# Three points per unit for the side work of loops 0 and 2, and an earlier route for the last group but one

## The chip, the cores and the metric

The kernel is one program on one core of a Trainium2 chip. Its time is the device time in microseconds (us) of that core. The engines are TensorE (PE in the profile, its weight loads PEld), VectorE (DVE), ScalarE (ACT), GpSimd (POOL) and the queue of SyncE (SP); they run in parallel, each executes its own instructions in order, and they wait for each other by semaphores.

## The reference

The input is x of 4 sequences x 1024 tokens x 128 channels. Six residual layers follow each other, each on a layer norm of x:

```
x = x + 0.5 * channel_mix(layernorm(x))          # RWKV-like, with the token before
x = x + attention(layernorm(x))                  # 16 heads of 8, rotary, softmax
x = x + 0.5 * channel_mix(layernorm(x))          # the same weights again
x = x + 0.5 * moe(layernorm(x))                  # 8 experts, top 2, hidden 256
x = x + linear_attention(layernorm(x))           # 16 heads of 8, causal sums, softplus
x = x + 0.5 * moe(layernorm(x))                  # the same experts again
```

moe: an RMS norm, router scores (tokens x 8), the two best experts with softmax weights, for each `(u * silu(gate)) @ w_down`, and the weighted sum plus the skip.

## The kernel before

**Tiles, groups, halves.** The 4096 tokens are 32 tiles of 128; 4 tiles are a group (8 groups), 4 groups a half (2 halves). x stays in on-chip memory all the time. Each of the two expert layers is worked in two halves, so there are four rounds r = 0 to 3 (r = 0 and 1 for the first layer, 2 and 3 for the second; the half is r % 2).

**One round.** First the *route*: `rroot` (VectorE: inverse roots of the variances, some 14 small operations in a chain), `rnorm` (VectorE: the normalised tokens xr, tile by tile), then for each group `rext` (TensorE transposes xr, ScalarE copies the result) and `rscore` (TensorE: router scores, VectorE copies them). With all four groups there come the *slots*: `rtop` 0 and 1 (VectorE: first and second expert), `rcount` (TensorE counts, VectorE copies and scans), `rscan`, `rplace` (VectorE: the slot of each token), `roff` (the expert of each slot tile) and `rweight`. Then 32 *scatters* (`scat`): GpSimd writes xr, tile by tile and twice, to its slots in HBM, sorted by expert (L1594). Then the *expert loop* of the round: 39 slot tiles, two per unit, so 20 units (`UNITS`), and three more passes to drain. Last 32 gathers (`gath`, L1604), which take the results back; they and the additions `cadd` lie in the next round's loop, or in the linear stage, or at the end.

**The expert loop** is software-pipelined over `UNITS + 3` = 23 passes. In pass u TensorE transposes unit u (L1649; it needs SyncE's load of the slots, three units ahead), does the up-projections of unit u - 1 (L1659), transposes the hidden values of unit u - 2 (L1671) and does the down-projection of unit u - 3 (L1685). VectorE copies and scales the transposed unit (L1726) and multiplies by the SiLU of unit u - 1 (L1733); ScalarE does SiLU (L1760) and the copies L1766 and L1773; SyncE stores unit u - 3 (L1828) and loads (L1822). All loads of a round wait on SyncE for all scatters of that round, and come behind the stores of the round before in its queue.

**Side pieces.** What doesn't belong to the experts is cut into pieces, and `plan_loop` writes out, before the program is built, which piece stands where: two places in a pass, `first` behind the transposition of unit u and `second` behind the up-projections. Every engine walks through the same plan and executes its own share of a piece in its place, so a piece on TensorE that needs VectorE's share of an earlier piece holds up all that TensorE has behind it. `turn_of(works, 4)` takes the next piece of each list of work at a place, with at most one piece for TensorE. All side pieces that use a PSUM bank use bank 1 (`SIDE_BANK`), one after the other.

Loop 0 carries, in this order: the end of the attention (`div`, `turn`, `proj`, `rest`, `stats`), `factors` and the channel mix of the last group (`side_mix(11)`: mn, mt, md, mx, mk, mr, mv, ms), then `route_part(1, 1, 8)` (root and norm of tiles 8 to 15 of the half, rext and rscore of groups 2 and 3), the slots of round 1 and its scatters, one per place; what is left at the last place goes there all together. By this plan rplace of round 1 stands in pass 12, and 12 of the 32 scatters stand in the last place. Loop 2 carries `route_part(3, 1, 8)`, the slots of round 3 and its scatters: rplace in pass 5, the last scatter in pass 21. `pool_follow` makes a gather or scatter wait for the transposition or up-projection of its place, in the drain passes only where there is one.

**The linear stage** (`plan_linear`, 132 steps) lies between loops 1 and 2, with a plan of its own; its `extra` pieces, at most one route piece per step, carry the route of round 2 and groups 0 and 1 of round 3. `spread` leaves empty steps behind some kinds. TensorE executes `extra` in front of the step's weighted sums (L1975), which ScalarE copies (L2169) for the division (L1917, L1922) of a later step. Its last `lstats` (the statistics of the last group) comes right before loop 2.

## Time and profile before

| | us |
|---|---|
| median of 3 runs | 1353.01 (1352.94 to 1354.49) |
| the profiled execution | 1355.71 |
| its span | 1353.80 |

| engine | busy us |
|---|---|
| TensorE matmul | 1091.2 |
| ScalarE | 806.7 |
| VectorE | 655.0 |
| GpSimd | 375.7 |

Times in the rows are counted from the span's start. Loop 0 begins near 668, loop 1 near 781, the linear stage near 860, loop 2 near 1146 and loop 3 near 1233. "Idle before <- releaser" says how long an engine sat before an instruction and what ended that; "issue" is a wait for nothing that the profile shows, "remote" or "another core or an unknown queue" one that it can't name. The granted clock of TensorE is given as a share: 1.00 is 2.4 GHz, 0.50 is 1.2 GHz, and a stretch between them is a mix of both.

### The profile page before, as it was taken

How to read it: one execution, taken by the hardware profiler on the slowest of the kernel's cores; microseconds unless marked ns; L12 is line 12 of the kernel's file. 1: busy time of each engine (PE TensorE's matmuls, PEld its weight loads, DVE VectorE, ACT ScalarE, POOL GpSimd, SP SyncE). 2: the span in 40 equal slices, each digit the busy share in tenths (PEclk: the TensorE clock that was granted, in tenths of full speed). 3: DMA queues.
4: the chain of work that ended last, by engine and by line, in shares of the span. 5: the costliest groups of instructions: out<-in, count | busy, mean ns of one | idle time of the engine just before them, and what ended most of it. 6: DMA issues, size and time to landing. Idle time of an engine off the chain costs nothing.

```text
span 1353.8 us, 20967 instructions
## 1 busy us (share of the span) xinstructions
PE 1091.2 (81%) x7616; PEld 508.4 (38%) x7616; DVE 655.0 (48%) x2060; ACT 806.7 (60%) x1164; POOL 375.7 (28%) x376
## 2 busy tenths in 40 slices
PE   3459899989989999999879489877887777898940
PEld 2332222223222321232256356443544344565630
DVE  5742555464454340433165146567666662633522
ACT  4328778788887999989734345654443331364520
POOL 2100111112100102333002744144240363155535
PEclk8779989999999999999999789889788686898985
DMA  4450450450038301100012233100000011133522
GB/s 138 62 90 1 70 83 1 71 81 2 2 54 149 102 3 62 68 15 28 9 43 69 80 90 100 34 15 19 9 17 1 13 33 40 49 112 100 143 66 67
DMA packets 83411, 74.07 MB, mean 55 GB/s; under 512 B 11248, under 2 KB 77680, under 8 KB 82416
## 3 DMA queue, kind: packets, MB, share of 16 engines
q1 hardware_dynamic: 73824, 55.06, 18.8%
q0 software_dynamic: 8192, 16.79, 4.3%
q8 instruction: 66, 1.08, 0.4%
q10 hardware_dynamic: 1296, 0.86, 0.2%
q14 instruction: 33, 0.27, 0.1%
HBM read 39.26 MB, written 33.42 MB: 54 GB/s over the span
## 4 chain that ended last, share of the span: by engine, by line
PE 53%; DVE 20%; ACT 11%; issue 5%; POOL 3%; DMA 2%; another core or an unknown queue 1%; SPq 0%; POOLq 0%; DVEq 0%; ACTq 0%
PE ps L987 11%; PE ps L1659 9%; ACT attn_probs L1250 9%; PE ps L972 6%; PE ps L1685 4%; PE ps L590 3%; PE ps L881 2%; PE ps L1962 2%; PE ps L1671 2%; POOL moe_back L1604 2%; PE ps L1649 1%; PE ps L1886 1%; DVE lin_scores L2091 1%; DVE moe_xr L1105 1%; DVE room L1106 1%
## 5 line engine op out<-in xcount | busy, mean ns | idle before, releaser
L1250 ACT ACTIVATE attn_probs<-ps 128x1024 f32<-128x1024 f32 x512 | 486.1, 1083 | 91.3 <-PE ps L972 91.2
L987 PE MATMUL ps<-attn_probs,attn_v 128*18 128x512 f32 x2048 | 275.1, 610 | 1.9 <-DVE room L1217 1.3
L972 PE MATMUL ps<-stack 50*128 50x512 bf16 x1024 | 167.3, 391 | 17.6 <-DMA stack<-row_maxima 11.5
L1594 POOL DMA_INDIRECT slots<-moe_xr,moe_slot x128 | 124.9, 975 | 197.5 <-ACT attn_probs L1250 78.9
L1659 PE MATMUL ps<-stack,lin_scores 128*128 x312 | 155.4, 621 | 0.0
L1604 POOL DMA_INDIRECT moe_back<-results,moe_slot x128 | 123.6, 966 | 111.0 <-PE ps L1649 47.2
L972 PEld LDWEIGHTS ps<-stack 50*128 50x128 bf16 x1024 | 34.3, 94 | 255.5 <-ACT attn_probs L1250 228.8
L1760 ACT ACTIVATE lin_scores<-ps 128x256 f32<-128x256 f32 x156 | 58.4, 381 | 105.6 <-PE ps L1659 100.3
L1733 DVE TENSOR_TENSOR lin_scores<-ps,lin_scores 128x256 f32<-128x256 f32 x156 | 59.1, 419 | 105.0 <-ACT lin_scores L1760 85.3
L1685 PE MATMUL ps<-stack,lin_scores 128*128 x624 | 86.6, 283 | 10.3 <-ACT lin_heads_out L1773 6.8
L1685 PEld LDWEIGHTS ps<-stack,lin_scores 128*128 128x128 f32 x624 | 78.7, 198 | 12.2 <-issue 11.9
L1288 POOL TENSOR_TENSOR room<-room 128x512 f32<-128x512 f32 x16 | 24.5, 1530 | 190.4 <-DVE room L1082 190.4
L1659 PEld LDWEIGHTS ps<-stack,lin_scores 128*128 128x128 f32 x312 | 56.1, 201 | 40.1 <-issue 40.0
L1726 DVE TENSOR_SCALAR lin_scores<-ps,c_norm_scale 128x256 f32<-128x256 f32 x80 | 37.9, 474 | 56.2 <-PE ps L1649 49.7
L2091 DVE TENSOR_TENSOR lin_scores<-ps,c_causal 128x512 f32<-128x512 f32 x64 | 41.1, 684 | 49.4 <-PE ps L1962 46.7
L2161 ACT ACTIVATE lin_scores<-ps 128x512 f32<-128x512 f32 x64 | 34.8, 595 | 45.7 <-PE ps L1962 45.5
L987 PEld LDWEIGHTS ps<-attn_probs,attn_v 128*18 128x18 f32 x2048 | 34.8, 96 | 71.8 <-issue 48.4
L1082 DVE SCALAR_TENSOR_TENSOR room<-ps,c_attn_b,moe_xr 128x512 f32<-128x512 f32 x32 | 23.7, 748 | 78.6 <-PE ps L881 77.1
L1649 PE MATMUL ps<-c_ident,moe_gathered 128*128 128x128 f32 x156 | 33.5, 297 | 29.1 <-DMA moe_gathered<-slots 17.3
L1766 ACT ACTIVATE lin_scores<-ps 128x512 f32<-128x512 f32 x80 | 46.7, 584 | 15.2 <-PE ps L1671 9.7
L1671 PEld LDWEIGHTS ps<-c_ident,lin_scores 128*128 128x128 f32 x312 | 39.4, 144 | 37.5 <-issue 36.5
L1773 ACT ACTIVATE lin_heads_out<-ps 128x256 f32<-128x256 f32 x80 | 30.1, 377 | 37.2 <-PE ps L1685 22.4
(237 smaller groups left out, 1584.4 us busy)
## 6 DMA issues: line engine op xcount, KB each, us to landing
stack<-qk_parts SPq DMA_DIRECT2D x48, 256.0 KB, 9.2
moe_gathered<-slots SPq DMA_DIRECT2D x76, 128.0 KB
results<-lin_heads_out SPq DMA_DIRECT2D x76, 128.0 KB
slots<-zeros SPq DMA_DIRECT2D x2, 2496.0 KB, 14.9
qk_parts<-moe_xr SPq DMA_DIRECT2D x32, 128.0 KB, 5.2
qk_parts<-moe_xr SPq DMA_DIRECT2D x16, 192.0 KB, 2.8
stack<-in_expert_w SPq DMA_DIRECT2D x1, 3072.0 KB
x<-in_x SPq DMA_DIRECT2D x8, 256.0 KB, 8.4
```

The source lines that it names most:

```text
L972: instruction = T.matmul(k.ps[:, SCORE_BANKS[i % 3][s], :], d.stack[b % 2][rows, 1, pair, kt * P:(kt + 1) * P], d.stack[b % 2][rows, 0, pa ...
L987: instruction = T.matmul(k.ps[32 * j:32 * j + STRIP, PV_BANK, :], d.v[:, b % 2, kt, first:first + STRIP], d.probs[:, n % A_PROBS, j * BANK ...
L1250: A.activation(d.probs[:, n % A_PROBS, 2 * e * BANK:2 * (e + 1) * BANK], k.ps[:, banks[0]:banks[1] + 1, :].rearrange("p a n -> p (a n)"), ...
L1594: G.indirect_dma_start(out=k.dram["slots"][half], out_offset=bass.IndirectOffsetOnAxis(ap=d.slot[:, s, at, c:c + 1], axis=0), in_=d.xr[:, ...
L1604: G.indirect_dma_start(out=k.back[:, at % RING, c, :], out_offset=None, in_=k.dram["results"][half], in_offset=bass.IndirectOffsetOnAxis(a ...
L1649: instruction = T.transpose(k.ps[:, bank, i * P:(i + 1) * P], k.moe.gathered[:, u % NG, i, :], k.ident[:, :])
L1659: T.matmul(k.ps[:, bank, :], d.gt[:, u % NB, i, :], w[:, bass.ds(offset[u, i], 2 * HIDDEN)], start=True, stop=True).then_inc(k.full[bank], 1)
L1671: instruction = T.transpose(k.ps[:, bank, at:at + P], d.h[:, u % NB, i, c * P:(c + 1) * P], k.ident[:, :])
L1685: instruction = T.matmul(k.ps[:, bank, i * DIM:(i + 1) * DIM], d.ht[:, u % NB, i, c * P:(c + 1) * P], w[:, 2 * HIDDEN + c * DIM:][:, bass. ...
L1733: V.tensor_tensor(d.h[:, u % NB, i, :], k.ps[:, bank, 0:HIDDEN], d.silu[:, u % NB, i, :], ALU.mult).then_inc(k.free[bank], 1)
L1760: A.activation(d.silu[:, u % NB, i, :], k.ps[:, bank, HIDDEN:2 * HIDDEN], ACT_FN.Silu).then_inc(k.e_silu, 1)
L2091: V.tensor_tensor(d.scores[:, m % NS, :].rearrange("p (j t) -> p j t", j=HPG), k.ps[:, bank, :].rearrange("p (j t) -> p j t", j=HPG), caus ...
```

## The change

Loops 0 and 2 get three places per pass for the pieces: the third stands behind the transposition of the hidden values, in front of the down-projection, on TensorE and ScalarE; VectorE and SyncE execute it right behind the second. Loops 1 and 3 keep two. Scatters stay at the first two places. In loop 0 the route of group 2 of the half becomes a work list of its own that starts behind `proj`, beside the last mix; group 3 comes behind the mix, each with its own root (4 tiles). In the linear stage group 2 of round 3 gets its route behind `lstats` of group 6, and loop 2 starts with the route of group 3 alone. By the new plan rplace of round 1 stands in the second place of pass 7 and 3 scatters in the last place that takes any; in loop 2 rplace stands in the third place of pass 2 and the last scatter in pass 18. `rnorm` now names its first and last tile.

```diff
-SIDE_BANK = 1
+SIDE_BANK, PLACES = 1, 3
...
-    yield OTHER, ("rnorm", r, part)
+    yield OTHER, ("rnorm", r, part * TPB, (part + 1) * TPB)
...
+def route_group(r, g):
+
+    yield OTHER, ("rroot", r, g * TPG, (g + 1) * TPG)
+    yield OTHER, ("rnorm", r, g * TPG, (g + 1) * TPG)
+    yield PRODUCT, ("rext", r, g)
+    yield PRODUCT, ("rscore", r, g)
...
+        if ("lstats", GROUPS - 2) in out:
+            routes += spread(route_group(3, HALF_GROUPS - 2))
...
-    slots = [[] for _ in range(2 * (UNITS + 3))]
+    places = [[[] for _ in range(PLACES)] for _ in range(UNITS + 3)]
+    slots = [place for unit in places for place in unit[:2]]
...
-        works = [list(route_part(3, 1, TPB)) + list(route_slots(3))]
+        works = [list(route_group(3, HALF_GROUPS - 1)) + list(route_slots(3))]
...
+    for n, out in enumerate(place for unit in places for place in unit) if r % 2 == 0 else ():
+        out += turn_of(works, 4)
+        if n % PLACES < 2:
+            out += scatters if n // PLACES == UNITS + 2 and n % PLACES else scatters[:1]
+            scatters = scatters[1:]
+        if ("stats", BATCH - 1, HALVES - 1) in out:
+            works.insert(0, [(OTHER, ("factors", TILES - TPG, TILES))] + list(side_mix(SIDE_MIXES - 1)))
+        if ("proj", BATCH - 1, HALVES - 1) in out:
+            works.append(list(route_group(1, HALF_GROUPS - 2)))
+        if ("ms", SIDE_MIXES - 1) in out:
+            assert not works
+            works.append(list(route_group(1, HALF_GROUPS - 1)) + list(route_slots(1)))
+        if ("rplace", r + 1) in out:
+            scatters = transfers("scat", r + 1)
     for n, out in enumerate(slots):
-        if r == 0 or r == 2:
-            out += turn_of(works, 4)
-            out += scatters if n == len(slots) - 1 else scatters[:1]
...
-            if ("ms", SIDE_MIXES - 1) in out:
-                works.append(list(route_part(1, 1, TPB)) + list(route_slots(1)))
...
-            for at in range(piece[2] * TPB, (piece[2] + 1) * TPB):
+            for at in range(piece[2], piece[3]):
...
@@ TensorE, and ScalarE likewise: def pe_loop, def act_loop
-        first, second = k.e_plan[r][u]
+        first, second, third = k.e_plan[r][u]
...
             turn_hidden(u - 2)
+        for piece in third:
+            side(piece)
         if 0 <= u - 3 < UNITS:
             down(u - 3)
...
@@ VectorE, and SyncE likewise: def dve_loop, def sp_loop
-        for piece in second:
+        for piece in second + third:
             side(piece)
```

## Rows read from the trace of the kernel before

**Rows 1.** The page, busy time, share of the span and instructions of each engine.
```profile
PE 1091.2 (81%) x7616; PEld 508.4 (38%) x7616; DVE 655.0 (48%) x2060; ACT 806.7 (60%) x1164; POOL 375.7 (28%) x376
```

**Rows 2.** Table by stretch: length; busy PE, PEld, DVE, ACT, POOL; clock, DMA share, GB/s.
```profile
667.89:756.33 88.44, 76.39 (x387) 53.20 (x388) 47.70 (x168) 39.00 (x93) 19.27 (x20) 0.92 0.21 58
756.33:780.91 24.58, 4.96 (x31) 3.72 (x29) 0.70 (x2) 2.68 (x7) 16.64 (x18) 0.65 0.24 77
1124.00:1146.45 22.45, 16.52 (x117) 11.93 (x117) 3.87 (x15) 3.58 (x6) 7.64 (x9) 0.61 0.16 47
1146.45:1223.39 76.94, 67.28 (x350) 45.35 (x350) 38.80 (x130) 38.62 (x92) 29.28 (x31) 0.91 0.27 79
1223.39:1232.68 9.29, 4.45 (x30) 3.31 (x29) 0.71 (x2) 2.72 (x7) 2.79 (x3) 0.93 0.36 105
```

**Rows 3.** Chain of waits behind loop 0: start, duration, what.
```profile
765.55 3.81 another core or an unknown queue
769.69 0.33 SPq L1828
770.09 8.72 issue
```

**Rows 4.** Timeline of GpSimd, loop 0: start, duration, instruction, idle before it.
```profile
733.66 1.18 POOL L1594 DMA_INDIRECT slots<-moe_xr,moe_slot  x1 [32.96 <-DVE moe_slot L1510]
741.13 0.95 POOL L1594 DMA_INDIRECT slots<-moe_xr,moe_slot  x1 [1.24 <-remote]
762.68 0.96 POOL L1594 DMA_INDIRECT slots<-moe_xr,moe_slot  x1 [0.30 <-issue]
776.57 0.95 POOL L1594 DMA_INDIRECT slots<-moe_xr,moe_slot  x1 [0.30 <-issue]
```

**Rows 5.** Timeline of TensorE, loop 0.
```profile
707.78 0.66 PE L590 MATMUL ps<-c_ident,moe_xr 128*128 128x128 f32 x4 [2.62 <-DVE moe_xr L1456]
708.27 2.75 PE L1659 MATMUL ps<-stack,lin_scores 128*128 x4
725.40 0.23 PE L1419 MATMUL ps<-moe_both,before_bf 128*128 128x128 bf16 x1 [1.74 <-DVE moe_both L1481]
749.90 0.38 PE L1649 MATMUL ps<-c_ident,moe_gathered 128*128 128x128 f32 x2
750.12 1.88 PE L1659 MATMUL ps<-stack,lin_scores 128*128 x4
753.17 0.27 PE L1649 MATMUL ps<-c_ident,moe_gathered 128*128 128x128 f32 x1
```

**Rows 6.** Timeline of VectorE, loop 0.
```profile
703.03 0.16 DVE L1445 TENSOR_SCALAR moe_root_var<-moments 128x8 f32<-128x8 f32 x1
706.62 2.14 DVE L1456 TENSOR_SCALAR moe_xr<-x,moments,moe_root 128x128 f32<-128x128 f32 x8
723.44 0.28 DVE L1472 TENSOR_REDUCE moe_top<-moe_scored 128x16 f32<-128x128 f32 x1
725.26 0.17 DVE L1482 TENSOR_TENSOR moe_gap<-moe_top 128x16 f32<-128x16 f32 x1
```

**Rows 7.** Timeline of VectorE, then of TensorE, end of the linear stage.
```profile
1126.91 0.20 DVE L2042 TENSOR_TENSOR lin_total<-ps,lin_total 128x36 f32<-128x36 f32 x1 [2.15 <-remote]
1131.59 2.40 PE L1975 MATMUL ps<-lin_scores,lin_v 128*9 128x128 f32 x32
```

**Rows 8.** Timeline of TensorE, start of loop 2.
```profile
1154.42 1.11 PE L590 MATMUL ps<-c_ident,moe_xr 128*128 128x128 f32 x4 [3.20 <-DVE moe_xr L1456]
1155.32 3.62 PE L1659 MATMUL ps<-stack,lin_scores 128*128 x4
1158.74 1.42 PE L1410 MATMUL ps<-router_scaled,moe_xrt 128*128 128x8 f32 x8
1169.39 0.23 PE L1419 MATMUL ps<-moe_both,before_bf 128*128 128x128 bf16 x1 [1.74 <-DVE moe_both L1481]
```

**Rows 9.** Timeline of TensorE, seam behind loop 2.
```profile
1227.00 1.15 PE L1685 MATMUL ps<-stack,lin_scores 128*128 x8 [1.02 <-issue]
```

More of the change, by code:

```diff
@@ L474, in plan_loop @@
     scatters = []
-    for n, out in enumerate(slots):
-        if r == 0 or r == 2:
-            out += turn_of(works, 4)
-            out += scatters if n == len(slots) - 1 else scatters[:1]
-            scatters = scatters[1:]
-            if ("stats", BATCH - 1, HALVES - 1) in out:
-                works.insert(0, [(OTHER, ("factors", TILES - TPG, TILES))] + list(side_mix(SIDE_MIXES - 1)))
-            if ("ms", SIDE_MIXES - 1) in out:
-                works.append(list(route_part(1, 1, TPB)) + list(route_slots(1)))
-            if ("rplace", r + 1) in out:
-                scatters = transfers("scat", r + 1)
-        elif r == 1 and ("lnorm", 0) in [piece for one in slots[:n] for piece in one]:
+    for n, out in enumerate(place for unit in places for place in unit) if r % 2 == 0 else ():
[12 more added lines that the diff above has]
+            scatters = transfers("scat", r + 1)
+    for n, out in enumerate(slots):
+        if r == 1 and ("lnorm", 0) in [piece for one in slots[:n] for piece in one]:
             if k.l_more[0][1][0] not in ("lexp", "lln") or n >= 2 * (UNITS + 1):
                 out.append(k.l_more.pop(0)[1])
-    assert not works and (r != 2 or ("rweight", 3) in [piece for one in slots for piece in one])
-    plan = [(slots[2 * u], slots[2 * u + 1]) for u in range(UNITS + 3)]
-    k.e_plan[r] = plan
+    assert not works and (r % 2 or ("rweight", r + 1) in [piece for unit in places for one in unit for piece in one])
+    k.e_plan[r] = places
     for u in range(UNITS + 3):
-        first, second = plan[u]
+        first, second, third = places[u]
         if u < UNITS:
@@ L506, in plan_loop @@
             k.banks.fill(("eht", r, u - 2), 6)
+        for piece in third:
+            if key := bank_key(piece):
+                k.banks.fill(key, SIDE_BANK)
         if 0 <= u - 3 < UNITS:
@@ L1704, in pe_loop @@
             turn_hidden(u - 2)
+        for piece in third:
+            side(piece)
         if 0 <= u - 3 < UNITS:
@@ L1736, in dve_loop @@
     for u in range(UNITS + 3):
-        first, second = k.e_plan[r][u]
+        first, second, third = k.e_plan[r][u]
         if u < UNITS:
@@ L1776, in act_loop @@
     for u in range(UNITS + 3):
-        first, second = k.e_plan[r][u]
+        first, second, third = k.e_plan[r][u]
         for piece in first:
@@ L1785, in act_loop @@
             turn_hidden(u - 2)
+        for piece in third:
+            side(piece)
         if 0 <= u - 3 < UNITS:
@@ L1839, in sp_loop @@
     for u in range(UNITS + 3):
-        first, second = k.e_plan[r][u]
+        first, second, third = k.e_plan[r][u]
         if u + AHEAD < UNITS:
@@ L1846, in sp_loop @@
             store(u - 3)
-        for piece in second:
+        for piece in second + third:
             side(piece)
```

## The prediction

> **What bounds the kernel now.** I read the page's line of busy shares first: TensorE is busy 81% of the span, so a microsecond in which it waits in order is lost unless something else hides it [rows 1]. Then the table by stretches, for the two loops that change [rows 2]. Loop 0 runs from its first transposition (667.89) to its last pair of up-projections (756.33), 88.44 us for 20 units; loop 2 takes 76.94 us for the same 20. A unit without a stall takes 3.27 us, the distance of two starts of L1649 [rows 5], so 20 take 65.4: loop 0 carries 23.0 us of stalls, loop 2 11.5. Third, the seam behind each loop: 24.58 us from the last up-projections of loop 0 to the first transposition of loop 1, with TensorE busy 4.96 of them; behind loop 2 the seam is 9.29 us [rows 2]. The chain of waits says what the longer seam waits for: 8.72 us from 770.09, which end at 778.81 when the gather of loop 1 is issued [rows 3]. That gather needs every scatter of the second half, and GpSimd issues the last at 776.57, one each 1.263 us since 762.68 ((776.57 - 762.68) / 11) [rows 4]: twelve scatters have no place left in the loop and stand in its last one. Loop 2 has none left over.
>
> **The change, part by part.** By the lists of both plans, the last placing of the route (rplace) of loop 0 moves from unit 12 to unit 7, its 32 scatters begin at unit 8 instead of 12 and still go two per unit; 3 instead of 12 are left in the last place. In loop 2 rplace moves from unit 5 to 2 and the last scatter from unit 21 to 18. I sum against the profiled execution, 1355.71 us (span 1353.80 and 1.91 around it); it is 2.70 above the median of 1353.01, so I add the sum to the median.
>
> *A. The seam of loop 0.* Nine scatters fewer at its end, 9 x 1.263 = 11.4 us [rows 4]. Behind them comes a second limit: ScalarE's last three copies of the down-projection end waits of up to 3.8 us put down to an unknown queue, while scatters are issued without a pause [rows 3]. The last store leaves at 769.7, 9.1 us before the gather of 778.81; if those waits stay whole, the gather can't come earlier than about 770.1 in the old clock of events, which is 8.7. The pauseless stream now ends at about 766, so the third wait should shrink. Gain 8.6 to 11.4; I take 10.0.
>
> *B. The length of loop 0.* The work moved is the same, but each engine executes in order, and a unit now holds three links of a chain that crosses engines. TensorE meets the same waits with fewer units between them to cover them. The present waits of the route: 2.62 us before L590, 1.74 before L1419 [rows 5]. Now by hand. Unit 1 has, on VectorE, one root (2.9 us: from 703.03 to the rnorm at 706.62, less a multiplication of 0.7 [rows 6]), a multiplication with SiLU, the statistics, and half of an rnorm (1.1 us, half of 2.14 [rows 6]) before TensorE's rext of the same unit: TensorE, free at about 676.4, waits until 681.3, and the mix of the last group, whose factors come behind that on VectorE, is transposed at 686.8 instead of 684.2. From there the mix has three places per unit and gains: its last TensorE step comes at 696.0 instead of 697.6, but in unit 4 and not 6. The last group's root and rnorm then hold rext to 705.8 (a wait of 3.4), and unit 6 begins at 709.1, or at 710.8 if TensorE falls to its lower clock behind the wait, as it did behind the 2.62: L1659 took 2.75 us there for four matmuls that take 1.88 otherwise [rows 5]. In unit 6 TensorE needs both tops before rcount: 0.4 + 0.5 + 1.95 + 0.7 + 1.85 = 5.4 us from the unit's start (a top is 723.44 to 725.43 [rows 6]), though it has only 2.8 us of its own work before it. From there VectorE is the bound for two units: rcount, rscan, rplace and roff are about 6.6 us, with two transposed copies and one multiplication between them 8.2, so unit 9 begins 13.6 us after unit 6, 722.8 to 724.5. Eleven units of 3.27 and the stall behind the first five scatters (GpSimd itself sat 1.24 us at 741.13 [rows 4]; 1.1 us of the unit, kept) bring the last up-projections to 759.9 to 761.6 instead of 756.33. First scatter: near 722.5, not 733.66. Loss 3.6 to 5.3; bounds 2.0 (all later waits half as long) and 6.5 (each wait over 2.6 us costs a stretch of the lower clock too); I take 4.6.
>
> *C. The linear stage.* It gets root, rnorm, rext and rscore of the last group but one, 1, 3, 6 and 8 steps behind the statistics. VectorE is idle 2.15 us before L2042 at 1126.91 and its consumer on GpSimd stands behind a scatter until 1128.2, so root and rnorm are hidden [rows 7]. TensorE's are not: rext falls into the run of L1975 at 1131.59 that ScalarE's next copy waits for, rscore into the run behind it, and TensorE is at its lower clock in this stretch (granted 0.61, near half [rows 2]). The lower-clock prices are 1.1 us (L590) and 1.42 (L1410) [rows 8]. Cost 2.5; bounds 0 (both fit into idle time of TensorE, of which the 22.45 us have 5.9) and 3.0.
>
> *D. The length of loop 2.* Gone is the second rext and rscore, which stood in a unit only 0.7 us over the plain one. Added is the same crowding, and here the chain starts cold. rext runs at 1154.4 as before, but then come turn(1) (0.65) and rscore (1.42) before the first up-projections, which start at 1157.7 instead of 1155.32 and end near 1160.7. VectorE can only then multiply (1161.9) and take both tops (3.9): rcount goes at 1165.9, and TensorE, having only one transposition in between, waits 5 us; before, it had units 2 and 3 there and waited 1.74, at 1169.39 [rows 8]. rcount thus comes 3.5 us earlier in time and two units earlier in work (6.5 us). Behind it VectorE runs multiplication, rscan, rplace and turn(3) until 1174.5, which holds turn(4). A stall-free unit 4 would have been reached at 1174.5 - 4 x 3.27 = 1161.4 on the scale of unit 0; before, the same scale stands at 1156.8 when the route is through. Cost 4.7; bounds 1.5 (VectorE's small operations slip between, no lower clock) and 5.5.
>
> *E. The seam of loop 2.* The last nine scatters now are long done, so the 1.02 us that TensorE sat before L1685 at 1227.00 [rows 9] should go. Gain 0.7; bounds 0 and 1.0.
>
> Loops 1 and 3, the fourth variable in the plan and the rnorm's new arguments issue the same instructions: nothing. All else that moves (ScalarE's copies of rext, 0.6 us each) lies in its idle time, 49 of 88 us in loop 0 [rows 2].
>
> Sum: -10.0 + 4.6 + 2.5 + 4.7 - 0.7 = +1.1 us: 1356.8 as a profiled execution, 1354.1 as a median.
>
> The clock belongs in B and D. The row shows half-rate matmuls after a wait of 2.62 us (2.75 for 1.88) [rows 5] and after one of 3.2 us (3.62 [rows 8]). The Trainium skill, page "TensorE: Matmul & The Clock Gate", section "Loop structure matters more than you think", says that long waits between matmuls drop the engine to its half rate, and that the loop nest decides it; it speaks against a change that trades many short waits for few long ones, and this trace agrees. With full rate behind every wait B and D would be about 1.7 and 1 us smaller and the sum -1.6.
>
> GpSimd's first scatter, beside VectorE's roff, lasted 1.18 us and the others 0.95 to 0.96 [rows 4]. The Trainium skill, "DMA: Bandwidth & Descriptors", section "SWDGE vs HWDGE vs iDMA", says that VectorE in one of its modes can lock GpSimd out of the memory where it writes its descriptors. Fewer scatters now lie behind the last VectorE route step, so this could only shorten A's stream, by 0.2 us.
>
> **Rivals.** *The waits are covered.* The seam gives its full measure and the crowding little: A -10.7, B +2.0, C +1.0, D +1.5, E -0.7, together -6.9: 1346.1. For it: loop 0 is 23.0 us over plain units, and part of that is one chain that three places run faster. Against it: no added place gives VectorE any time, and in unit 11 it was already the one waited for.
>
> *TensorE's in-order wait for rcount* (slower). In both loops it stands one place behind the second top, with 2.4 to 5 us of nothing under it, and each such wait brings the lower clock: B +6.5, C +3.0, D +5.5, with A at -8.6 and E at -0.4, together +6.0: 1359.0. It decides as soon as B + C + D exceed the seam by 2.7, that is 13.4. For it: L1659's 3.62 us behind the wait at loop 2's start. Against: the wait of 1.74 had no slow matmuls behind it.
>
> *The seam isn't the scatters'* (the change doesn't do what it says): the unexplained waits of ScalarE grow with the loop's later end and eat A down to 5: sum +6, the same time as the last.
>
> **How the numbers follow.** About 0.2%, 2.7 us, is what a measurement of this kernel tells from no change. The forecast has 0.42 (0.34 within 2.7 us, 0.03 faster, 0.05 slower), the covered waits 0.31 (0.29 faster, 0.02 within), the rcount wait 0.20 and the seam's failure 0.07 (0.25 slower, 0.02 within). Faster 0.32, same 0.38, slower 0.30. The forecast's own range is 1350 to 1358; with the two sides down to 1345.5 and up to 1360.5 some 0.2 is left out.
>
> **What would show it.** Last scatter of loop 0 at about 770 and the first transposition of loop 1 at 774 to 778 (A and B together); the last up-projections at 760 to 762 (B); a wait over 2.3 us before L1419 in both loops (B, D); the linear stage's end at 1149 less the shift of before (C); loop 2 near 81.6 us (D). Wrong it would be if L590 in unit 1 of loop 0 waits under 3 us, or if the seam behind loop 0 stays above 18 us.

## The result, and the profile after

The changed kernel takes 1359.49 us (median of 8 runs, 1358.14 to 1366.59), the kernel before beside it 1354.41 (8 runs, 1351.61 to 1359.86): ratio 1.0038, 95% interval 1.0020 to 1.0057. It is slower by 0.4%, 5.1 us by the medians. The forecast was 1354.1 and a sum of +1.1 us; its own range was 1350 to 1358, and only the wide one, with the rivals' sides, reached to 1360.5. The profiled execution after took 1358.14 us, with a span of 1356.2 and a mean granted clock of 0.896, that of before 1355.71, 1353.8 and 0.896: +2.4 in both.

The table by stretches of the kernel after, with the columns of [rows 2]: loop 0, its seam, the end of the linear stage, loop 2 and its seam.

```profile
666.52:763.92 97.40, 81.47 (x387) 55.65 (x388) 51.65 (x184) 39.23 (x93) 27.78 (x29) 0.86 0.20 59
763.92:778.51 14.59, 4.76 (x30) 3.52 (x28) 0.71 (x2) 2.79 (x7) 8.06 (x9) 0.80 0.30 91
1119.83:1142.36 22.53, 15.82 (x128) 11.98 (x128) 7.55 (x34) 4.18 (x7) 7.33 (x8) 0.68 0.15 47
1142.36:1226.18 83.82, 69.73 (x339) 45.78 (x339) 37.92 (x125) 37.88 (x91) 31.97 (x33) 0.86 0.26 75
1226.18:1234.66 8.48, 4.45 (x31) 3.31 (x29) 0.70 (x2) 2.69 (x7) 0.00 (x0) 0.94 0.29 84
```

Against [rows 2] these rows show a trade between stages: loop 0 is 8.96 us longer (97.40 for 88.44), its seam 9.99 shorter, loop 2 6.88 longer (83.82 for 76.94), its seam 0.81 shorter. The end of the linear stage, from its last group of score matmuls to loop 2, took 21.98 us before (1124.47 to 1146.45) and takes 22.53. The rest, which the prediction put at nothing, gave 3.6 back: 1.37 ahead of loop 0, 2.07 in loop 1 (74.77 to 72.70) and 0.17 in the rest of the linear stage; loop 3 and the end took 0.42. Together +2.4. The five stages that the change touches add up to +5.6.

In loop 0 TensorE does the same 387 matmuls, but in 81.47 us and not in 76.39: the granted clock of the stretch fell from 0.92 to 0.86. In loop 2 it does 339 for 350, since a group's route has left, and yet is busy 69.73 us for 67.28, at a clock of 0.86 for 0.91. TensorE's timeline in loop 0, at the last group's route:

```profile
699.99 1.88 PE L1676 MATMUL ps<-stack,lin_scores 128*128 x4
705.43 1.12 PE L607 MATMUL ps<-c_ident,moe_xr 128*128 128x128 f32 x4 [3.56 <-DVE moe_xr L1473]
711.30 3.60 PE L1676 MATMUL ps<-stack,lin_scores 128*128 x4
718.05 0.23 PE L1436 MATMUL ps<-moe_both,before_bf 128*128 128x128 bf16 x1 [2.72 <-DVE moe_both L1498]
718.18 2.05 PE L1702 MATMUL ps<-stack,lin_scores 128*128 x8
720.44 2.44 PE L1676 MATMUL ps<-stack,lin_scores 128*128 x4
724.27 1.88 PE L1676 MATMUL ps<-stack,lin_scores 128*128 x4
```

The four up-projections of a unit (L1676) take 1.88 us at full clock. Behind the wait of 3.56 us they take 3.60, and the down-projections (L1702) 2.05 for 1.06. The granted clock is 0.50 over the 9.28 us from 705.43 to 714.71 and 0.63 over the 4.55 us behind the second wait, and 1.00 only from 722.73 on. Loop 2's start shows the same, and answers to [rows 8]:

```profile
1150.23 1.11 PE L607 MATMUL ps<-c_ident,moe_xr 128*128 128x128 f32 x4 [7.24 <-DVE moe_xr L1473]
1153.82 3.76 PE L1676 MATMUL ps<-stack,lin_scores 128*128 x4
1162.60 0.29 PE L1436 MATMUL ps<-moe_both,before_bf 128*128 128x128 bf16 x1 [4.59 <-DVE moe_both L1498]
1162.80 3.78 PE L1676 MATMUL ps<-stack,lin_scores 128*128 x4
```

The extension (L607, the transposition of the route's xr) waits 7.24 us where TensorE waited 3.48 before unit 1's transposition at 1150.56 and 3.20 before the extension; that is 0.6 us more. The count (L1436) waits 4.59 where it waited 1.74. The count is 6.8 us earlier in time, 2.7 if counted from the loop's first transposition, and yet loop 2 takes longer.

### The profile page after: what moved, and what is told of

It is laid out like the page before. It is cut to its first block, busy times and chain, and to the rows that moved or that the text cites. A ratio compares the mean times of both kernels' runs of the same rounds, so it can differ in the third digit from the quotient of the medians.

```text
span 1356.2 us, 20999 instructions
## 1 busy us (share of the span) xinstructions
PE 1095.4 (81%) x7616; PEld 509.6 (38%) x7616; DVE 661.7 (49%) x2092; ACT 807.1 (60%) x1164; POOL 376.5 (28%) x376
## 3 DMA queue, kind: packets, MB, share of 16 engines
q8 instruction: 66, 1.08, 0.4%
## 4 chain that ended last, share of the span: by engine, by line
PE 53%; DVE 21%; ACT 11%; issue 5%; POOL 3%; DMA 2%; another core or an unknown queue 1%; SPq 0%; POOLq 0%; DVEq 0%; ACTq 0%
PE ps L1004 11%; PE ps L1676 9%; ACT attn_probs L1267 9%; PE ps L989 6%; PE ps L1702 4%; PE ps L607 3%; PE ps L898 2%; PE ps L1983 2%; POOL moe_back L1621 2%; PE ps L1688 2%; PE ps L1666 2%; PE ps L1907 1%; DVE lin_scores L2112 1%; DVE moe_xr L1122 1%; PE ps L1943 1%
## 5 line engine op out<-in xcount | busy, mean ns | idle before, releaser
L989 PE MATMUL ps<-stack 50*128 50x512 bf16 x1024 | 167.5, 391 | 17.5 <-DMA stack<-row_maxima 11.4
L1676 PE MATMUL ps<-stack,lin_scores 128*128 x312 | 159.5, 635 | 0.0
L1702 PE MATMUL ps<-stack,lin_scores 128*128 x624 | 85.8, 281 | 8.8 <-issue 4.9
L1702 PEld LDWEIGHTS ps<-stack,lin_scores 128*128 128x128 f32 x624 | 77.8, 196 | 10.5 <-issue 10.5
L1676 PEld LDWEIGHTS ps<-stack,lin_scores 128*128 128x128 f32 x312 | 57.6, 206 | 41.3 <-issue 41.2
L607 PE MATMUL ps<-c_ident,room 128*128 128x128 f32 x132 | 25.9, 329 | 29.2 <-DVE room L596 18.2
```

The costliest lines, as they stand in the source:

```text
L607: instruction = T.transpose(k.ps[:, bank, i * P:(i + 1) * P], source(i), k.ident[:, :])
L989: instruction = T.matmul(k.ps[:, SCORE_BANKS[i % 3][s], :], d.stack[b % 2][rows, 1, pair, kt * P:(kt + 1) * P], d.stack[b % 2][rows, 0, pa ...
L1676: T.matmul(k.ps[:, bank, :], d.gt[:, u % NB, i, :], w[:, bass.ds(offset[u, i], 2 * HIDDEN)], start=True, stop=True).then_inc(k.full[bank], 1)
L1702: instruction = T.matmul(k.ps[:, bank, i * DIM:(i + 1) * DIM], d.ht[:, u % NB, i, c * P:(c + 1) * P], w[:, 2 * HIDDEN + c * DIM:][:, bass. ...
```

## Experiments

Experiment 5 is the kernel before and experiment 9 the changed one; the others are edits of the changed one. Experiments 1 to 4 ran on the chip numbered 7, 5 to 8 on chip 15, 9 to 12 on chip 0; "the first chip" means where the profiles of before and after shown so far were taken. No number is on record for it: that it was a fourth chip, and not one of these at another time, is inferred from its times and not shown. Lengths of a loop are given in this section from its first transposition to that of its unit 19, and "gap" is from there to the first transposition of the next loop, since both ends are single rows of TensorE's timeline. "Idle" is the length of a loop less TensorE's busy time in it. A profile is one execution, and a loop whose plan is unchanged can differ by some 3 us between two of them (last section). "..." in the code marks lines left out.

**1. Three places in loop 0 alone, with group 2's route beside the last mix.** Loop 2 has two places and its old route, and nothing is moved into the linear stage:

```
-        if ("lstats", GROUPS - 2) in out:
-            routes += spread(route_group(3, HALF_GROUPS - 2))
...
-        works = [list(route_group(3, HALF_GROUPS - 1)) + list(route_slots(3))]
+        works = [list(route_part(3, 1, TPB)) + list(route_slots(3))]
...
-        out += turn_of(works, 4)
+        if n % PLACES < {0: 3, 2: 2}[r]:
+            out += turn_of(works, 4)
```

> Only loop 0 takes three places per pass, with the route of group 2 beside the mix; loop 2 and the linear stage are planned as before. My theory (each loop's pieces stall TensorE by themselves, and only loop 0 gets something back at its seam): loop 0 is 9.0 us longer as in the changed kernel, the seam 10.0 shorter, loop 1 some 2 shorter, loop 2 76.9 us as before. Time within 4 us of the kernel before, ratio 0.997 to 1.001. Rival (three places cost the same everywhere and the seam gains nothing real): loop 0 alone 4 to 6 us slower than before.

Measured: 1341.72 us for 1341.03, ratio 1.0002 (0.9988 to 1.0017). Loop 0 takes 93.29 us, its gap 16.47, where experiment 5 has 83.69 and 27.70 for the kernel before: what the seam gives, the loop takes, within 1.6 us. Loop 0's half of the change is worth nothing as written.

**2. The other half: three places in loop 2 and the route moved into the linear stage.** Loop 0 as before.

> Only loop 2 takes three places per pass, with the last but one group's route in the linear stage; loop 0 is planned as before. My theory: loop 2 is 83 to 84 us instead of 76.9, its seam 0.8 shorter, the linear stage's end 0.5 longer: 5 to 7.5 us slower than before (ratio 1.004 to 1.0055), more than the whole change. Rival (the loss sits in loop 0): within 2 us of before.

Measured: 1358.38 us, ratio 1.0120 (1.0093 to 1.0147). The loss is here, 17.4 us, more than twice the 5 to 7.5 expected, and on this chip three times the 0.4% of the first measurement. Loop 2 takes 79.34 us, and from loop 1's unit 19 to loop 2 it takes 291.78, where experiment 1 has 69.87 and 284.31: the expectation had taken 0.5 us for the linear stage from the first chip's profiles.

**3. Both routes moved, two places everywhere.**

```
-        out += turn_of(works, 4)
+        if n % PLACES < {0: 2, 2: 2}[r]:
+            out += turn_of(works, 4)
```

> Both loops keep two places per pass, but the route of the last but one group is its own work: beside the mix in loop 0, in the linear stage for loop 2. rplace comes one pass earlier in each (pass 11 and 4), 10 instead of 12 scatters at the last place of loop 0. If the third place is what costs (my theory), loop 0 stays within 2 us of 88.4 and loop 2 within 1.5 us of 76.9, the seam is 2.5 us shorter: 0 to 4 us faster than before. Rival (the added root and the moved rext in VectorE's and TensorE's order are what costs, whatever the places): 2 to 5 us slower than before.

Measured: 1348.46 us, ratio 1.0065 (1.0039 to 1.0091). That is 7.4 us slower, outside what either theory allowed. Without a third place anywhere about half of the loss is there: 296.10 us from loop 1's unit 19 to loop 2, where experiment 1, without the moved route, has 284.31. Of these 11.8 us 7.5 lie in the stage's last stretch, which experiment 6 takes apart; the other 4.3 lie before it, where nothing was moved, and no other profile has them.

**4. The changed kernel with idle identity matmuls in TensorE's waits.** Their results are overwritten by the piece behind them; 10 to 20 of them stand ahead of an extension, 8 or 14 ahead of a count.

```
+            filler(piece, k.use[piece], {(1, 2): 14, (1, 3): 10, (3, 3): 20}.get((r, g), 0))
             T.wait_ge(k.e_xr, HALF_GROUPS * r + g + 1)
+            filler(piece, k.use[piece], {1: 8, 3: 14}.get(r, 0))
             T.wait_ge(k.e_both, r + 1)
```

> The changed kernel, with matmuls of the identity put into TensorE's waits of loops 0 and 2 (14 and 10 before rext of groups 2 and 3 of loop 0, 8 before its rcount, 20 before rext of loop 2, 14 before its rcount); their results are overwritten. Clock theory: half of the loss is the lower clock behind the waits (in loop 0 TensorE is busy 81.5 us for the 387 matmuls that take 76.4 before), so the granted clock of loop 0 rises from 0.86 to over 0.93, and of loop 2 from 0.86 to over 0.92, and the kernel is 4 to 8 us faster than the changed one, near the kernel before. [...]

Measured: 1351.94 us, ratio 1.0071 (1.0045 to 1.0097). The clock did rise. Loop 0 of this kernel, then of experiment 1, whose loop 0 is the same without the filling; then loop 2 of this kernel and of experiment 2:

```profile
672.19:764.77 92.58, 82.18 (x435) 58.49 (x436) 50.82 (x181) 36.33 (x85) 25.72 (x26) 0.91 0.21 59
```

```profile
669.20:762.49 93.29, 77.36 (x371) 53.15 (x372) 50.76 (x181) 36.48 (x85) 25.79 (x26) 0.87 0.21 59
```

```profile
1144.72:1222.11 77.39, 70.67 (x389) 50.39 (x389) 37.01 (x122) 35.30 (x83) 31.92 (x33) 0.95 0.27 79
```

```profile
1143.94:1223.28 79.34, 65.56 (x321) 43.50 (x321) 37.09 (x122) 35.30 (x83) 31.90 (x33) 0.86 0.26 77
```

The granted clock goes from 0.87 to 0.91 in loop 0 (over 0.93 was expected) and from 0.86 to 0.95 in loop 2, the loops only from 93.29 us to 92.58 and from 79.34 to 77.39. The idle matmuls are 7.63 and 8.47 us of the busy time. Without them TensorE's own matmuls take 2.8 and 3.4 us less than unfilled, and its waits, those that are filled counted with them, 2.1 and 1.4 more: over half of what the clock gives back goes into waits. I take it that VectorE's chain, which the clock doesn't shorten, sets the pace there; in loop 2 the wait for VectorE before the transposition at 1172.58 is 1.88 us for 1.22 in experiment 2. The Trainium skill, page "Perfetto Trace Analysis", section "Matmul Optimizations", asks for matmuls back to back in batches, since the engine scales its power with its use; these rows agree on the clock.

By the medians the filling does more: 6.4 us under experiment 2 (1351.94 for 1358.38), although this kernel carries experiment 1's half too; the expected gain over the changed kernel was 4 to 8. The execution profiled is the slowest of the six (1356.39). Between the 2.7 us of the two loops' rows and the 6.4 of the medians the size of the gain stays open.

**5. The kernel before, profiled on the chip of experiments 6 to 8.**

> The kernel before, unchanged, profiled on the chip of the three kernels that follow, so that their stages can be read against it. Both theories: loop 0 from its first transposition to unit 19's 84 to 86 us, its seam 27.5 to 28, loop 2 70 to 74, its seam 11.6 to 12.5, as in the profiles at hand; the stretch from loop 1's unit 19 to loop 2's first transposition 284 us if this chip is like that of the first four experiments, 294 if it is like the first chip.

Measured: one run of 1337.25 us, span 1335.3, clock 0.904; loop 0 83.69, gap 27.70; loop 1 69.28, then 284.24 to loop 2; loop 2 69.93, gap 11.52. The first chip's profile of the same program has 85.28, 27.74, 71.61, 293.93, 73.78 and 12.45. Of 18.5 us between the two spans 9.7 lie between loop 1's unit 19 and loop 2, nearly all of them in the last stretch of the linear stage (21.98 for 12.51), and 3.9 in loop 2; the seam of loop 0 takes the same.

**6. The moved route of group 2 alone.** Two places in both loops, loop 0's route as before; only the two lines of experiment 1's diff that put the route into the linear stage are left in, and the loop 2 that starts with the last group.

> Before, with one edit alone: the route of group 2 of round 3 moved into the end of the linear stage (two places in both loops, loop 0's route as before). Theory (the moved route stands in the chain of the last divisions, where TensorE, VectorE and ScalarE are all waited for): the end of the linear stage grows by 6 to 8 us on a chip whose end is short before and by 0.5 to 2.5 us on one whose end is long, and loop 2 gains at most 1 us from having one group less; ratio 1.003 to 1.007. Rival (the moved route is nearly free, and what beside_only lost came from loop 0's half of the edit): stretch from loop 1's unit 19 to loop 2 within 2 us of before's, ratio 0.999 to 1.001.

Measured: 1346.52 us for 1339.29, ratio 1.0056 (1.0039 to 1.0074). The place is the end of the linear stage. The stretch from the last L1962 or L1982 to loop 2's first transposition, first before, then with the route moved:

```profile
1119.85:1132.36 12.51, 9.25 (x115) 6.99 (x114) 3.98 (x14) 3.12 (x6) 7.79 (x9) 1.00 0.19 61
```

```profile
1124.51:1144.60 20.09, 16.80 (x127) 12.98 (x127) 7.30 (x34) 3.71 (x7) 7.31 (x8) 0.61 0.17 53
```

It is 7.58 us longer and TensorE's busy time grows by 7.55, so its waits together don't grow (3.26 us before, 3.29 then). The twelve added matmuls are 1.12 + 1.85 us of it, and the other 4.6 are the same 115 matmuls at a lower clock, granted 0.61 where it was 1.00. The same stretch takes 12.51 to 12.59 us in all seven profiles from these three chips in which the route isn't moved, and 20.07 to 20.09 in all five in which it is. The timelines show where the clock came down, before and then with the edit:

```profile
1125.96 0.51 PE L1917 MATMUL ps<-lin_state,stack 128*128 128x144 f32 x2
1126.75 1.08 PE L1922 MATMUL ps<-c_head_rows,lin_sums 128*128 128x36 f32 x8 [0.28 <-ACT lin_sums L2169]
```

```profile
1129.40 1.12 PE L606 MATMUL ps<-c_ident,moe_xr 128*128 128x128 f32 x4 [1.93 <-DVE moe_xr L1472]
1133.93 1.85 PE L1426 MATMUL ps<-router_scaled,moe_xrt 128*128 128x8 f32 x8
1137.55 0.85 PE L1937 MATMUL ps<-lin_state,stack 128*128 128x144 f32 x2
1138.33 1.92 PE L1942 MATMUL ps<-c_head_rows,lin_sums 128*128 128x36 f32 x8
```

Before, TensorE has no wait over 0.8 us there until the gather's; with the edit it waits 1.93 us for VectorE's root and rnorm, and everything behind runs at 0.85 for 0.51 and 1.92 for 1.08, with a granted clock of 0.50 over the 15.2 us up to loop 2. The first slow row is the extension itself, 1.12 us for four transpositions that take 0.66 at full clock, so it was down when the wait ended. That the wait brought it down is read from this order; no run fills that wait.

Loop 2 takes 72.78 us for 69.93 although a group is gone from it. TensorE waits 3.5 us there for VectorE's copy of a transposition, 3.1 for the extension and 2.7 for the count, where it waited 2.1, 3.2 and 1.7: the group that is gone had covered part of the chain. The execution profiled was one of the two slowest (1352.46); 4.6 us of it lie ahead of loop 0.

**7. Three places in loop 2 alone, no route moved.**

> Before, with one edit alone: loop 2 takes side pieces at three places in a pass; no route is moved, loop 0 is as before. Theory (each wait of TensorE for a side piece loses the units that used to cover it): loop 2 grows by 7 to 9 us and its seam gives back 1, ratio 1.004 to 1.006; that is no less than in the changed kernel, since the pieces of group 2 come within the first two units. Rival (loop 2's loss in the changed kernel comes from the moved route, which leaves rank and count with less before them): loop 2 within 2 us, ratio 0.999 to 1.002.

Measured: 1348.91 us, ratio 1.0071 (1.0049 to 1.0092). Loop 2 takes 79.92 us for 69.93, its gap is 11.66 for 11.52: all of the loss, and not the 1 us expected back. The loop in this kernel, then in the kernel before (experiment 5):

```profile
1130.63:1210.55 79.92, 69.63 (x333) 46.19 (x333) 37.72 (x126) 35.95 (x84) 29.40 (x31) 0.83 0.27 78
```

```profile
1132.36:1202.29 69.93, 62.16 (x333) 42.39 (x334) 37.03 (x126) 36.00 (x84) 26.76 (x28) 0.95 0.30 87
```

Of the 10.0 us only 2.5 are idle time of TensorE. The other 7.5 are the same 333 matmuls at a granted clock of 0.83 for 0.95.

**8. Loop 0 as in experiment 1, with idle places ahead of what TensorE waits for.**

```
+def rested(pieces, rests):
+
+    out = []
+    for piece in pieces:
+        out += [(OTHER, ("rest",))] * rests.get(piece[1][0], 0) + [piece]
+    return out
...
+            works.append(rested(route_group(1, HALF_GROUPS - 2), {"rext": 2}))
+            works.append(rested(list(route_group(1, HALF_GROUPS - 1)) + list(route_slots(1)), {"rext": 2, "rcount": 2}))
```

> The changed kernel's loop 0 (three places, group 2 beside the mix), with idle places put ahead of the three pieces for which TensorE waited there: two ahead of each extension and two ahead of the count. Loop 2 and the linear stage as before. Theory (the waits are lost only because TensorE reaches the piece before its data, with other units' work behind it): 5 to 8 us of the 11 us of waits are filled with units' work, the scatters begin 1 to 3 us later, and the seam grows by 0 to 3 us; against the same kernel without the rests 3 to 6 us less, ratio to before 0.995 to 0.999. Rival (what loop 0 lost is the lower clock and the extra load on VectorE, not the waits): loop 0 within 2 us of the 93.3 us of the kernel without rests, seam longer, ratio 1.000 to 1.003.

Measured: 1335.18 us for 1339.29, ratio 0.9980 (0.9958 to 1.0001). Loop 0 is 84.90 us, 8.4 less than in experiment 1, from six places that hold nothing. And the first scatter, planned one unit later, is issued 55.2 us behind the loop's first transposition and not 59.7 (723.45, and 728.88 in experiment 1). Its gap is 18.82. I read it so: a TensorE that stands in a wait holds up the units that VectorE has to multiply between the route's steps, and the waits delayed their own chain. Loop 0 in this kernel and in the kernel before (experiment 5), to be read beside experiment 1's in experiment 4:

```profile
668.28:753.18 84.90, 72.04 (x370) 49.09 (x371) 50.27 (x181) 36.38 (x85) 23.80 (x24) 0.92 0.22 63
```

```profile
667.45:751.14 83.69, 72.65 (x370) 50.77 (x371) 46.89 (x165) 36.28 (x85) 17.30 (x17) 0.92 0.20 58
```

Neither theory has it alone. From the kernel before to experiment 1 the loop grows by 4.9 us of idle time and 4.7 of matmul time, at a clock of 0.87 for 0.92. The idle places take back 3.1 of the first and 5.3 of the second. One long wait stays, now ahead of the last mix's transposition (6.85 us at 685.40).

**9. The changed kernel itself, on a third chip.**

> The changed kernel itself, on the chip of the three kernels that follow. Theory (the price of the moved route depends on what the end of the linear stage looks like on the chip: where the stage's last scores-to-loop-2 stretch of before is 12.5 us long, it costs 7 us and more; where it is 22 us long, as on the first chip, it costs 0.5): on a chip whose stretch from loop 1's unit 19 to loop 2 is 284 us before, this kernel shows 291 to 293, loop 2 79 to 80, loop 0 with its seam about before's, and the ratio is 1.006 to 1.011. Rival (the 1.0038 of the first measurement is what the change costs anywhere): 1.002 to 1.0057 again.

Measured: 1355.88 us for 1336.04, ratio 1.0150 (1.0127 to 1.0173): the stages came where they were expected, the whole above the 1.006 to 1.011, part of it by loop 1. Against experiment 5, whose chip has the same time for the kernel before within 0.3%: loop 0 +9.8, its gap -11.3, loop 1 +2.2, the stretch to loop 2 +7.6, loop 2 +9.4, its gap 0.0, ahead of loop 0 -0.7, the rest +0.2; together 17.3, the difference of the spans (1352.6 and 1335.3).

**10. Loop 0 as in experiment 1, three scatters per pass.**

```
-            out += scatters if n // PLACES == UNITS + 2 and n % PLACES else scatters[:1]
-            scatters = scatters[1:]
+            count = len(scatters) if n // PLACES == UNITS + 2 and n % PLACES else 2 if r == 0 and n % PLACES == 0 else 1
+            out += scatters[:count]
+            scatters = scatters[count:]
```

> The changed kernel's loop 0 alone (three places, group 2 beside the mix; loop 2 and the linear stage as before), with three of round 1's scatters issued per pass instead of two. Theory (what ends the seam is now ScalarE's last copies and the store of the last unit, not the scatters): seam as before this edit, 16 to 17.5 us, loop 0 93 to 94, ratio 0.999 to 1.001. Rival (the spacing of the scatters still sets the seam, since the last one starts at the end of the passes): the last scatter starts 5 us earlier and the seam is 12 to 14 us, ratio 0.996 to 0.998.

Measured: 1332.56 us for 1336.04, ratio 0.9977 (0.9961 to 0.9993). I had read the seam as ended by ScalarE's last copies, and that was wrong here: the gap is shorter than both theories had it. The last scatter starts at 768.57, 5.6 us behind unit 19's transposition and not 12.0 as in experiment 9, and the gap falls from 16.4 to 11.43, with loop 0 at 93.54. Only now do the copies end it: the chain has the last one at 771.53 and the gather at 772.26, and the gap is about that of loop 2, 11.5 to 11.7. What misled me is visible in two profiles of the same kernel. The chain of waits at the end of the seam, the changed kernel on the first chip and then in experiment 9:

```profile
768.84 3.14 another core or an unknown queue
772.01 0.38 ACT lin_heads_out L1792
772.39 3.13 another core or an unknown queue
775.55 0.29 ACT lin_heads_out L1792
...
776.28 2.18 DMA moe_gathered<-slots
```

```profile
768.82 0.29 ACT lin_heads_out L1792
...
771.05 0.95 POOL slots L1611
772.01 0.30 issue
772.31 2.22 DMA slots<-moe_xr,moe_slot
774.53 0.02 issue
774.55 2.07 DMA moe_gathered<-slots
```

In both fences the left column is the start, then the duration. On the first chip ScalarE's last copy comes at 775.55 behind two unexplained waits, on the other at 768.82, and there the last scatter's landing releases the gather.

**11. The idle places and three scatters per pass together.**

> The kernel with idle places ahead of the extensions and the count in loop 0, with three scatters per pass instead of two. The profile of that kernel has its first scatter 55.2 us behind the loop's first transposition and its last one 99.5 us, against 94.3 us if they followed one another at 1.263 us each. Theory (the passes are now done before the scatters are, so the scatters end this seam): the stretch from loop 0's first transposition to loop 1's falls from 103.7 to 99 to 101 us, ratio 0.993 to 0.997. Rival (the last copies and the gather's landing end the seam here too): within 1 us of 103.7, ratio 0.997 to 1.000.

Measured: 1327.03 us for 1336.04, ratio 0.9927 (0.9901 to 0.9953), the best version, 0.7% under the kernel before. Loop 0 is 84.91 us, the gap 13.92, together 98.8; the kernel before has 111.4 in experiment 5. Of these 12.6 us the medians show 9.0; in the profile loop 1 takes 2.7 back, 71.96 here and 69.28 there. The 32 scatters follow one another at 1.265 us on average, with no pause up to the gather, so GpSimd's stream sets the end:

```profile
760.94 0.96 POOL slots L1619
761.90 0.31 issue
762.21 2.22 DMA slots<-moe_xr,moe_slot
764.43 0.02 issue
764.45 2.15 DMA moe_gathered<-slots
```

**12. The same with three places and idle places in loop 2 too** (three ahead of the first extension, one ahead of the count).

> As the kernel before it, and loop 2 with three places in a pass too, its route where it was before, with three idle places ahead of the first extension and one ahead of the count. Theory (in loop 2 as in loop 0 three places cost only where a piece is reached before its data): loop 2 falls from the 79.9 us of three places without rests to 68.5 to 70.5, and its seam is 11.5 to 11.7: with the kernel before it 0 to 2 us less, ratio 0.991 to 0.997. Rival (loop 2 is bound by VectorE's chain of roots, keys and counts at its start, whatever stands ahead of it): loop 2 72 to 76 us, that is 2 to 5 us slower than the kernel before it, ratio 0.997 to 1.001.

Measured: 1331.09 us, ratio 0.9952 (0.9929 to 0.9974). Loop 2 takes 71.22 us, between the two theories: the idle places take 8.7 of the 10 us back that three places cost in experiment 7, and what is left is still 1.4 over experiment 11, with two, which one profile each doesn't tell apart. With them the count stands in the first place of pass 4 again, where it stood with two places, so little is left of the earlier route. Its seam gains nothing. The other 2.7 us against experiment 11 lie in unit 3 of loop 0 (9.8 for 7.2), which issues the same work. They are the clock; this kernel, then experiment 11:

```profile
690.08 3.76 PE L1685 MATMUL ps<-stack,lin_scores 128*128 x4
```

```profile
689.68 1.96 PE L1684 MATMUL ps<-stack,lin_scores 128*128 x4
```

With the router scores ahead of them (1.76 for 1.03) and the mix's matmuls behind (1.31 for 1.02) that makes 2.8 us.

## Why the prediction held, and which of its steps did not

The forecast of +1.1 us came near the measured span difference of +2.4 by luck. Its five terms measured +5.6 together, and what brought the profile back to +2.4 is 2.07 us of loop 1 and 1.37 ahead of loop 0, which the change doesn't touch. By the medians the difference is 5.1, the time of 1359.49 lies above the forecast's own range, and it is nearest to the count-wait rival's 1359.0. Term by term the forecast was good in two and wrong in three. Of its signs the wait before the count (2.72 and 4.59, over 2.3) came; the last scatter (772.81 for 770), loop 1's first transposition (778.51 for 774 to 778), the last up-projections (763.92 for 760 to 762), loop 2's length (83.82 for 81.6) and the first scatter (726.43 for 722.5) came late.

*A, the seam of loop 0: right.* -10.0 was forecast and -9.99 measured; on the chip of experiment 9 -11.3, near the full 11.4 of nine scatters. ScalarE's copies ended the seam on the first chip as forecast, and the third of their waits shrank, from 3.81 to 3.13 us; in the other profiles there is none of them.

*B, loop 0: the mis-sized term.* +4.6 within 2.0 to 6.5 was forecast, +8.96 measured, +9.8 elsewhere. The mechanism was as described and the first waits were met closely: 4.91 us before the extension at 679.76, against the 4.9 of the hand timeline, and 3.56 against 3.4. But the half rate that came with the first wait had been charged nothing: the next up-projections (683.36) take 3.76 us, and the mix of the last group is transposed at 686.91 where, counted from this loop's start, 685.4 was forecast. The second extension is 1.0 us late by it (705.43 for 704.4), and unit 6 begins at 710.87 where 707.7 to 709.4 was forecast, the half rate having reached the unit before it too. And "unit 9 begins 13.6 us after unit 6" was 16.5: that sum took VectorE's operations alone, but the up-projections between the two tops ran for 3.60 us at half rate, and VectorE stood 1.58 us for them, the down-projections and the next up-projections cost 1.6 more. I had charged the clock once, behind the second wait, and it had to be charged behind all three. Experiments 1 and 5 give its share: 4.7 of 9.6 us.

*C, the linear stage: wrong, hidden in the first measurement.* +2.5 within 0 to 3.0; +0.55 on the first chip, 7.5 to 7.6 in all profiles of the others. The step that failed there is "root and rnorm are hidden": it rested on VectorE's idle 2.15 us [rows 7], a wait put down to "remote" that stands beside a stall of TensorE and that experiment 5's profile doesn't have. The stall:

```profile
1125.61 0.51 PE L1917 MATMUL ps<-lin_state,stack 128*128 128x144 f32 x2
1129.74 1.92 PE L1922 MATMUL ps<-c_head_rows,lin_sums 128*128 128x36 f32 x8 [3.62 <-issue]
```

The stall of 3.62 us and the half rate behind it (1.92) were in the profile I read, at a granted clock of 0.60 over 21.98 us; on a chip without that stall the same matmuls take 12.51 us at 1.00. On the first chip the root and rnorm did fit beneath the stall, by then 5.06 us, and the clock came back for some 3 us behind it (0.68 for 0.60), so TensorE was busy 15.82 us for 16.05 in spite of the added matmuls: that is luck of the execution. Where the stretch isn't stalled the route costs its own matmuls, 3.0 us at half rate, and 4.6 us of half rate for the others. I took the stalled one for the kernel's own.

*D, loop 2: mis-sized as B was.* +4.7 within 1.5 to 5.5; +6.9, and +9.4 elsewhere. The wait of 5 us for the count was forecast and is 4.59. The extension comes where it was put, 7.9 us behind the loop's first transposition as before; the count comes 20.2 us behind it for a forecast of 19.4, the 0.8 being up-projections at half rate for all of 3.76 us. Behind the count the forecast had full rate again, and they take 3.78 there; unit 4 begins 29.8 us behind the first transposition for 28.1. The last 0.4 us of the 2.2 I can't place. It is the same fault as in B, a second wait whose clock was not charged; by experiment 7 three quarters of loop 2's loss are the clock. And [rows 8] was read too far: the 3.62 us of L1659 don't show what a wait of 3.2 us does, since TensorE was at half rate before it (two transpositions in 0.63 us at 1146.45, for 0.38 at full clock).

*E, the seam of loop 2: right at the first chip* (-0.8 for -0.7), and nothing elsewhere (11.57 for 11.52), where the seam of before is 0.9 us shorter already.

*Loops 1 and 3 at nothing: right.* Loop 1 gave 2.07 us, but in these profiles it takes either 69.1 to 70.0 or 71.2 to 72.0 us, and the kernel before has both (69.28, 71.61), the changed one too (69.54, 71.46). I take it that it is not the change's; what sets the two lengths is open.

Of the rivals, the wait for the count on TensorE is the one that came nearest: it had B +6.5, C +3.0 and D +5.5, and experiment 9 against 5 gives 9.8, 7.6 and 9.4, each larger than my upper bound (experiments 6 and 7 give 7.6 and 10.0 for C and D alone). It was right that each such wait brings the lower clock, but the waits for the extension are the longer ones, 4.91, 3.56 and 7.24 us for 2.72 and 4.59. The Trainium skill's rule on waits and half rate ("TensorE: Matmul & The Clock Gate", "Loop structure matters more than you think"), which I had charged at 2.7 us over B and D, bears more, and behind the waits of 2.7 us and more the traces agree with it: the same matmuls at the lower clock are 4.7 us of 9.6 in loop 0, 7.5 of 10.0 in loop 2 (experiment 7) and 4.6 of 7.6 in the linear stage (experiment 6).

## What to carry to other kernels

More places for side work are worth nothing on an engine that executes in order if its pieces come before their data; in loop 0 idle places ahead of those pieces gave 8.4 us back and brought the first scatter, the end of the chain that was to be hastened, 4.5 us forward too. Price each new wait twice: once by its length, and once by the matmuls behind it at half rate, which were half of the loss in loop 0 and three quarters in loop 2. When a chain's end is released by a stream of equal issues, pace the stream by the engine that issues it and not by the loop's places. Before a move into a stretch is priced by the idle time that one profile shows there, ask whether that idle time is the kernel's or a stall of that execution: if its clock is near half and a wait ends in "issue", the price elsewhere can be another.

## What the runs showed of the hardware

The clock moves a loop from one execution to the next. In experiment 7 and then 5 the same plan of loop 0 runs behind the same wait:

```profile
708.21 0.66 PE L604 MATMUL ps<-c_ident,moe_xr 128*128 128x128 f32 x4 [2.63 <-DVE moe_xr L1470]
708.71 1.88 PE L1673 MATMUL ps<-stack,lin_scores 128*128 x4
```

```profile
706.92 0.66 PE L590 MATMUL ps<-c_ident,moe_xr 128*128 128x128 f32 x4 [2.62 <-DVE moe_xr L1456]
707.41 3.01 PE L1659 MATMUL ps<-stack,lin_scores 128*128 x4
```

In the first the engine stays at full clock, in the second it falls to half rate within the up-projections, and loop 0 takes 80.84 us and 83.69. A wait of 1.93 us was followed by half rate in experiment 6, one of 2.63 us here was not. Unit 3 of loop 0 in experiment 12 and loop 2 of experiment 8, planned as before and 2.7 us longer than in experiment 5, are of the same kind. A difference of less than 3 us in one loop, from one profile each, is no evidence by itself.

The same kernel before took 1354.4 us in the first measurement and 1336.0 to 1341.0 on chips 7, 15 and 0. Half of the difference sits in one stretch, the end of the linear stage: a wait of TensorE put down to "issue" while GpSimd issues scatters (3.62 us), and the half clock behind it. Counted by waits that end in an unknown ("remote") release on TensorE, ScalarE and VectorE, ahead of, in and behind the loops and at the end of the linear stage, the first chip's profiles have 14 with 33.9 us together (before) and 11 with 22.6 (after), the longest 6.25 and 7.71; the twelve profiles from the other three chips have none, with the same stream of scatters. What makes them is open, and so is whether it is the chip; no experiment ran there.

Idle matmuls raised the granted clock from 0.87 to 0.91 in loop 0 and from 0.86 to 0.95 in loop 2; the loops gained 0.7 and 2.0 us by one profile each.
